# Self-attention softmax: row sums by TensorE over unnormalised exponentials, scaling moved behind the value products

## The reference

```
Q, K, V = x @ w.T + bias, split into heads
S = einsum('hid,hjd->hij', K, Q) * 32 ** -0.5
delta = i - j
S = where(delta < 0, -inf, S) - delta
C = softmax(S, axis=-1)
attn = einsum('hij,hjd->hid', C, V)
out = attn @ o_w.T + o_b
```

## Time and profile before

| | us |
|---|---|
| time, median of 3 runs | 1968.17 (1965.84 to 1968.95) |
| profiled execution, its own time | 1968.37 |
| profiled execution, span | 1966.6 |
| TensorE busy | 1904.0 (97%) |
| VectorE busy | 1099.3 (56%) |
| ScalarE busy | 978.7 (50%) |
| GpSimd busy | 327.6 (17%) |

### The profile page before, as it was taken

One profiled execution on the slowest core, in us unless ns is written; L12 is line 12 of the kernel. 1 busy time (PEld: TensorE's weight loads), 2 busy tenths in 40 slices (PEclk: granted clock), 3 DMA queues, 4 the chain that ended last, 5 costly groups with the idle time before them and its releaser, 6 DMA issues. The chain is left out here.

```text
span 1966.6 us, 32109 instructions
## 1 busy us (share of the span) xinstructions
PE 1904.0 (97%) x10494; PEld 1596.6 (81%) x10494; DVE 1099.3 (56%) x2447; ACT 978.7 (50%) x2079; POOL 327.6 (17%) x238
## 2 busy tenths in 40 slices
PE   9999999999999989999999999999887899999998
PEld 6787888888888878878888888887665688999997
DVE  3567677677677756676776777676645631000003
ACT  3204676676576582055775775775645441122111
POOL 0300211211211213002112111211552300000001
PEclk9999999999999999999999999999999999999999
DMA  7651111111111145501111111111300907577552
GB/s 245 212 193 43 40 50 41 46 37 40 51 32 43 43 150 190 185 25 46 33 45 45 32 49 42 37 38 38 115 15 24 343 6 266 208 265 265 198 188 66
DMA packets 123281, 198.12 MB, mean 101 GB/s; under 512 B 12741, under 2 KB 62021, under 8 KB 119104
## 3 DMA queue, kind: packets, MB, share of 16 engines
q1 hardware_dynamic: 119040, 188.59, 28.8%
q10 hardware_dynamic: 2880, 4.55, 0.7%
q0 software_dynamic: 1280, 3.93, 0.6%
HBM read 151.50 MB, written 45.81 MB: 100 GB/s over the span
## 5 line engine op out<-in xcount | busy, mean ns | idle before, releaser
L861 DVE TENSOR_TENSOR crs_ptl<-crs_tp,crs_pth 128x512 fp32r<-128x512 f32 x512 | 352.7, 689 | 178.9 <-ACT crs_pth L688 178.2
L688 ACT ACTIVATE crs_pth<-crs_tp 128x512 fp32r<-128x512 f32 x504 | 301.6, 599 | 243.7 <-PE crs_tp L1088 240.6
L606 POOL TENSOR_TENSOR crs_vl<-crs_vraw,crs_vh 128x512 fp32r<-128x512 f32 x128 | 164.9, 1288 | 1072.6 <-ACT crs_vh L695 1072.6
L1079 PE MATMUL crs_ring<-crs_kh,crs_ql 128*128 128x512 f32 x512 | 234.0, 457 | 0.3 <-DVE crs_kl L865 0.3
L1098 PE MATMUL crs_ov<-crs_ptl,crs_vh 128*128 128x512 f32 x512 | 209.6, 409 | 9.3 <-DVE crs_ptl L861 7.0
L1079 PE MATMUL crs_ring<-crs_kh,crs_qh 128*128 128x512 f32 x512 | 202.2, 395 | 0.0
L1098 PE MATMUL crs_ov<-crs_pth,crs_vh 128*128 128x512 f32 x512 | 202.2, 395 | 0.0
L1079 PE MATMUL crs_ring<-crs_kl,crs_qh 128*128 128x512 f32 x512 | 201.2, 393 | 0.0
L1098 PE MATMUL crs_ov<-crs_pth,crs_vl 128*128 128x512 f32 x512 | 199.3, 389 | 0.0
L1088 PEld LDWEIGHTS crs_tp<-all_ident,crs_prob 128*128 128x128 f32 x1024 | 143.0, 140 | 68.8 <-ACT crs_more L677 4.2
L1088 PE MATMUL crs_tp<-all_ident,crs_prob 128*128 128x128 f32 x1024 | 195.0, 272 | 3.3 <-ACT crs_more L677 3.3
(11 more groups left out here) (284 smaller groups left out, 3337.1 us busy)
## 6 DMA issues: line engine op xcount, KB each, us to landing
moe_w<-in_L_ffn_w SPq DMA_DIRECT2D x48, 1024.0 KB, 12.8
v_scratch<-crs_more SPq DMA_DIRECT2D x64, 512.0 KB, 2.9
crs_vraw<-v_scratch SPq DMA_DIRECT2D x128, 256.0 KB, 2.8
ex_w<-in_L_ffn_w SPq DMA_DIRECT2D x16, 1024.0 KB, 13.8
crs_prob<-in_ctx SPq DMA_DIRECT2D x16, 512.0 KB, 4.6
crs_wo<-in_L_xattn_Wo SPq DMA_DIRECT2D x16, 512.0 KB, 4.1
moe_w<-in_L_ffn_sw SPq DMA_DIRECT2D x8, 1024.0 KB, 13.4
qry_wq<-in_L_xattn_Wq SPq DMA_DIRECT2D x16, 256.0 KB, 4.1
```

Source lines behind the costliest of these rows:

```text
L606: nc.gpsimd.tensor_tensor(vl[:, n % VR, :, :], vraw[:, :, :], vh[:, n % VR, :, :].bitcast(F32), ALU.subtract).then_inc(s["v_lo"], 1)
L688: act.activation(pth[:, k % PT, :], tp[k % PT][:, :], ACT.Copy).then_inc(s["pt_hi"], 1)
L861: v.tensor_tensor(ptl[:, k % PT, :], tp[k % PT][:, :], pth[:, k % PT, :].bitcast(F32), ALU.subtract).then_inc(s["pt_lo"], 1)
L1079: m = pe.matmul(ring[at % RING][:, :], a[:, t // RT, rows], w[:, n % KR, :], start=i == 0, stop=i == 2)
```

## The change

The exponentials are turned and multiplied with V as they are, without their norm. Their sums are made by TensorE: behind the value products of a half come the same products with a matrix of ones in place of V, in the same column tiles, into the other half of the output's bank (`r_ps`), so that each sum stands in all 32 rows of its head. `inverse`, `normalise` and the accumulator of the exponentials go. VectorE's new `output` takes the reciprocal of `r_ps` (128x256) and multiplies `o_ps` with it into `on`. ScalarE copies `on` to `oh`, and GpSimd makes `ol`. TensorE's transposes wait for the exponentials, and its value products for `output` of the index before.

```diff
+        ones = t.sb("ones", [P, HW])
+        rinv = t.sb("rinv", [P, RT, P])
+        on = [t.sb(f"on{q}", [P, RT, P]) for q in range(2)]
+
+        r_ps = o_bank[:, TQ:2 * TQ].rearrange("p (r n) -> p r n", r=RT)
...
+            nc.gpsimd.memset(ones[:, :], 1.0).then_inc(c, 1)
+            pool.wait_ge(c, 2)
...
-            def normalise(n, it):
-                heads = HC // (it + 1)
-                pool.wait_ge(s["inv_ok"], unit(n, it))
-                w = sc[n % 2][it][:, 0:heads, :]
-                nc.gpsimd.tensor_tensor(w, w, rsum[n % 2][it][:, 0:heads].unsqueeze(2).to_broadcast([P, heads, (it + 1) * P]), ALU.mult).then_inc(s["norm_ok"], 1)
-
             for n in range(N):
-                for it in range(RT):
-                    normalise(n, it)
+                pool.wait_ge(s["o_hi"], n + 1)
+                nc.gpsimd.tensor_tensor(ol[:, place(n), :, :], on[n % 2][:, :, :], oh[:, place(n), :, :].bitcast(F32), ALU.subtract).then_inc(s["o_lo"], 1)
...
-            def inverse(n, it):
-                v.wait_ge(s["exp_ok"], unit(n, it))
-                v.reciprocal(rsum[n % 2][it][:, :], rsum[n % 2][it][:, :]).then_inc(s["inv_ok"], 1)
-                if it == 1:
-                    v.wait_ge(s["inv_ok"], unit(n, it))
-                    w = sc[n % 2][it][:, HC // 2:HC, :]
-                    v.tensor_tensor(w, w, rsum[n % 2][it][:, HC // 2:HC].unsqueeze(2).to_broadcast([P, HC // 2, 2 * P]), ALU.mult).then_inc(s["norm2_ok"], 1)
-
-            def output_low(n):
-                v.wait_ge(s["o_hi"], n + 1)
-                v.tensor_tensor(ol[:, place(n), :, :], o_ps, oh[:, place(n), :, :].bitcast(F32), ALU.subtract).then_inc(s["o_lo"], 1)
+            def output(n):
+                v.wait_ge(s["o_ps"], unit(n, 1) * HC)
+                v.reciprocal(rinv[:, :, :], r_ps).then_inc(s["inv_ok"], 1)
+                v.wait_ge(s["inv_ok"], n + 1)
+                if n >= 2:
+
+                    v.wait_ge(s["o_lo"], n - 1)
+                v.tensor_tensor(on[n % 2][:, :, :], o_ps, rinv[:, :, :], ALU.mult).then_inc(s["norm_ok"], 1)
...
             scores(0, 0)
             scores(0, 1)
-            inverse(0, 0)
             for n in range(N):
                 if n < N - 1:
                     scores(n + 1, 0)
-                inverse(n, 1)
                 if n < N - 1:
                     scores(n + 1, 1)
-                    inverse(n + 1, 0)
                 if n in QUERY_BESIDE:
                     query(QUERY_BESIDE[n])
                 turned(n)
                 if n:
-                    output_low(n - 1)
+                    output(n - 1)
             residual(0)
-            output_low(N - 1)
+            output(N - 1)
             residual(1)
...
-                    m = act.activation(w, w, ACT.Exp, bias=nmax[n % 2][it][:, h:h + 1], accum_out=rsum[n % 2][it][:, h:h + 1])
+                    m = act.activation(w, w, ACT.Exp, bias=nmax[n % 2][it][:, h:h + 1])
...
             def output_high(n):
-                act.wait_ge(s["o_ps"], unit(n, 1) * HC)
-                act.activation(oh[:, place(n), :, :], o_ps, ACT.Copy).then_inc(s["o_hi"], 1)
+                act.wait_ge(s["norm_ok"], n + 1)
+                act.activation(oh[:, place(n), :, :], on[n % 2][:, :, :], ACT.Copy).then_inc(s["o_hi"], 1)
...
             def transposes(n, it):
-                pe.wait_ge(s["norm_ok"], unit(n, it))
-                if it == 1:
-                    pe.wait_ge(s["norm2_ok"], n + 1)
+                pe.wait_ge(s["exp_ok"], unit(n, it))
...
                 elif n:
-                    pe.wait_ge(s["o_lo"], n)
+                    pe.wait_ge(s["norm_ok"], n)
                 for j in range(it + 1):
                     for h in range(HC):
                         rows = slice(h * HW, (h + 1) * HW)
-                        m = pe.matmul(o_ps[rows, it, :], V[:, place(n), j, rows], cT[n % 2][it][:, j, h * P:(h + 1) * P], start=j == 0, stop=j == it)
+                        pe.matmul(o_ps[rows, it, :], V[:, place(n), j, rows], cT[n % 2][it][:, j, h * P:(h + 1) * P], start=j == 0, stop=j == it)
+                for j in range(it + 1):
+                    for h in range(HC):
+                        rows = slice(h * HW, (h + 1) * HW)
+                        m = pe.matmul(r_ps[rows, it, :], ones[:, :], cT[n % 2][it][:, j, h * P:(h + 1) * P], start=j == 0, stop=j == it)
                         if j == it:
                             m.then_inc(s["o_ps"], 1)
```

More of the change, by code:

```diff
@@ L1201, in selfattn @@
         sc = [[t.sb(f"sc{q}{i}", [P, HC, (i + 1) * P]) for i in range(RT)] for q in range(2)]
-        mx, nmax, rsum = ([[t.sb(f"{n}{q}{i}", [P, HC]) for i in range(RT)] for q in range(2)] for n in ("mx", "nmax", "rsum"))
+        mx, nmax = ([[t.sb(f"{n}{q}{i}", [P, HC]) for i in range(RT)] for q in range(2)] for n in ("mx", "nmax"))
         cT = [[t.sb(f"cT{q}{i}", [P, i + 1, HC * P]) for i in range(RT)] for q in range(2)]
@@ L1221, in selfattn @@
         names = ("var_ready", "root_ready", "xn_ready", "chain", "consts", "b_ld", "vo_ld", "wo_ld", "xT_ps", "xT_hi", "xT_lo", "w_hi", "w_lo",
-                 "q_ps", "q_ok", "k_ps", "k_ok", "v_ps", "v_ok", "xb_ok", "s_ps", "s_ok", "max_ok", "exp_ok", "inv_ok", "norm_ok", "norm2_ok",
+                 "q_ps", "q_ok", "k_ps", "k_ok", "v_ps", "v_ok", "xb_ok", "s_ps", "s_ok", "max_ok", "exp_ok", "inv_ok", "norm_ok",
                  "t_ps", "cT_ok", "cT2_ok", "o_ps", "o_hi", "o_lo", "out_ps", "out_ok")
@@ L1251, in _ @@
             nc.gpsimd.iota(decay[:, :, :], pattern=[[-P, RT], [1, TQ]], base=0, channel_multiplier=-1, allow_small_or_imprecise_dtypes=True).then_inc(c, 1)
-            pool.wait_ge(c, 1)
+            nc.gpsimd.memset(ones[:, :], 1.0).then_inc(c, 1)
+            pool.wait_ge(c, 2)
             nc.gpsimd.affine_select(out=decay[:, :, :], in_=decay[:, :, :], compare_op=ALU.is_ge, fill=NEG,
@@ L1311, in _ @@
             query(1)
-            v.wait_ge(s["consts"], 2)
+            v.wait_ge(s["consts"], 3)
             def scores(n, it):
```

## The result

The changed kernel takes 2008.87 us (median of 4 runs, 2007.20 to 2011.87) against 1968.41 us of the kernel before on the same chip: 1.0203 of its time, with a 95% interval of 1.0185 to 1.0220. The profiled execution took 2009.26 us with a span of 2007.5, 40.9 us more than that of the kernel before.

What follows compares the result with a forecast made beforehand. Self-attention was taken as bound by a chain between engines, none full. Loops +17.3, loop 0 -1.6, the end +1.4 and clock restarts +9.0 gave +26.1 on 1968.37 us: 1994.5, forecast 1994, range 1979 to 2001.

Steps and rivals of the forecast that it cites:

- the moved wait: ScalarE's `output_high(n-1)` now waits for VectorE's `output(n-1)`, behind `turned(n)`, with exponentials queued after it; said to decide.
- the ring: Self-attention loops: transposes, VectorE's output, `output_high`, exponentials, next transposes in one cycle; 64.6 us against 47.3, +17.3.
- 1.16 from the eight transposes to VectorE's copy: Time in each loop from TensorE's transposes (n, 1) to VectorE's `turned(n)`, claimed as 1.16 us.
- 0.28 us each: ScalarE's exponentials of 256 columns without the accumulator read: four in 1.12 us in place of 1.99.
- Six restarts: TensorE at its slow clock after idling in each turn from loop 2 on: six times 1.5 = 9.0 us.
- the reciprocal at 1.7 us: R, VectorE's reciprocal of 128x256 in `output`: 1.7 us from 6 ns a column, bounds 0.42 and 2.7 us.
- what stands behind `out(0)`: After `out(0)`: last index's sums 0.6 us and `out(2)` waiting some 0.8 us for the last output, +1.4.
- Rival (a): VectorE's reciprocal streams at 0.42 us and four clock restarts stay: +13.3, 1982 us; chance 0.20.
- Rival (b): VectorE's reciprocal costs 8 to 10 ns a column, 2.3 to 2.7 us: 1999 to 2002 us; chance 0.11.
- Rival (c): TensorE's clock stays at its upper level although it pauses: 1985.5 us; chance 0.10.
- Rival (e): TensorE's sums run one tile at a time, not four: 14.4 us more, 2008 us; chance 0.02.
- Rival (d): `output_high(n-1)` finds `norm_ok` already given, so loops last as long as TensorE's own work: 1965 us; chance 0.04.

Runs made afterwards that it cites:

- the bare wait: Kernel before plus one wait only: ScalarE's `output_high(n-1)` also waits until VectorE's `turned(n)` is done; 1988.44 us, 1.0100 of before.
- the reorderings: Changed kernel with ScalarE's `output_high(n-1)` behind `turned(n, 1)` and `key`: 1981.58 us; or VectorE's `output(n-1)` ahead of `turned(n)`, `query` last: 1982.59 us; or both: 1971.68 us.
- the run with the copy: Changed kernel with the reciprocal of 128x256 replaced by a copy of the same shape, outputs multiplied by the sums; 1998.61 us, 1.0140 of before.
- both reorderings: Changed kernel with VectorE's `output(n-1)` ahead of `turned(n)`, `query` last, and ScalarE's `output_high(n-1)` behind `turned(n, 1)` and `key`; 1971.68 us, 1.0017 of before.

## Why the prediction was wrong

Direction and mechanism were right: the moved wait decides, `output_high` waits for VectorE's output, and the ring is the one written out. The kernel with the bare wait and the reorderings show it from both sides. The size was not: +26.1 forecast, +40.9 in the profiled executions. What failed are terms of the sum. By step the missing 14.8 us are as follows; this is a comparison of the sum with the trace, and the run with `query` moved warns that a term taken away need not come back in the total:

- **VectorE's place in the ring.** The term "1.16 from the eight transposes to VectorE's copy" was taken from loop 4, which has no `query`. In loops 1 and 3 `query` stands ahead of `turned` and waits for the second half projection; 3.35 us in place of 1.16, 4.4 us over the two. The description of VectorE's order ahead of the prediction had `query` there. The run with `query` moved shows the 2.0 us in loop 1's turn, and nothing in the total.
- **Exponentials.** 0.28 us each, the lower bound, was taken; they cost 0.40 (1467.83 to 1469.42 for four). Six turns of 4 x 0.12: 2.8 us. The rows of copies were of another kind of instruction; halfway between the bounds would have been closer. The Trainium skill ("ScalarE: Activation LUTs", "Step-by-step: what each stage is for") gives 0.833 ns an element whatever the function. This trace agrees for the slope: four of 128 columns start 1.19 us ahead of the next instruction (1459.38 to 1460.57), four of 256 1.59, so 0.10 us for 128 columns.
- **The clock.** Six restarts were counted at 1.5 us. The two turns behind a key pay for the scores too (1.59 us at 1482.35 where they take 0.87), so they are nearer 2.2; together 1.5 us more. The seventh restart, at `out(0)`, was put at nothing without a reason: the last loop was summed to `out(0)`, and its pause (4.15 us) not carried into the clock. It cost 2.1 us (5.15 against 3.00).
- **Behind the stage.** The next stage starts 38.6 us later, the whole kernel ends 40.9 us later. 2.3 us are in the experts, whose instructions are the same, and whose slow stretches of the clock fall elsewhere (granted clock of 0.81 in 1676 to 1691 us, 0.89 at the same place before, 1636 to 1651). Why they fall elsewhere stays open. The changed kernel's group of the first expert products:

```profile
L2141 PE MATMUL moe_bank<-moe_bufT,moe_w 128*128 128x160 f32 x1024 | 146.4, 303 | 0.6 <-ACT moe_bufT L1973 0.6
```

The same group of the kernel before:

```profile
L2144 PE MATMUL moe_bank<-moe_bufT,moe_w 128*128 128x160 f32 x1024 | 145.3, 302 | 0.7 <-ACT moe_bufT L1976 0.7
```

- **The rest.** Loop 0 won 1.15 and not 1.6 us. 4.4 + 2.8 + 1.5 + 2.1 + 2.3 + 0.45 = 13.6; the remaining 1.2 us are small differences spread over the turns (the sums 0.66 us for 0.6, `output_high` 0.32 us ahead of the exponentials for 0.28).

Right were: the reciprocal at 1.7 us (1748 ns) from a difference of 12 ns between two tiny rows, which is luck in part, since rows of two columns scatter from 158 to 166 ns; the multiplication (424 ns for 0.41); the sums at full clock (0.66 for 0.6); the subtraction (724 for 742); what stands behind `out(0)` (+1.6 for +1.4); the slow clock in each turn from loop 2 on. The reading of the Trainium skill's repeat count ("VectorE: DVE Perf Modes", "First, the fixed hardware budget") as 2.3 us for the reciprocal is not borne out: 1748 ns. Rival (a), a streaming reciprocal, is the run with the copy, 1999 and not the 1982 of its sum, for the same missing terms. It also took an idle of 1.7 us for one that leaves the clock up, where the earlier trace rows shows that for 1.43 only; a pause of 1.51 us in the kernel with both reorderings was followed by the lower clock. Rival (b) asked for R above 2.3 and has the wrong cause. Rival (c), a clock that stays up, falls with the 0.67 to 0.87 granted. Rival (e), at 2008, has almost the measured time by accident: the sums take 0.66 us beside the value products' 0.79, so they do not run one tile at a time. Rival (d), the open ring at 1965, had its point right: with `norm_ok` given in time the loops cost what they did (47.45 for 47.28 us). It takes two changes of order, a changed end and four matmuls without use to get to 1965.18.

The range failed for the same reason as the sum. Its ends came from the prices (R, the clock), and no term stood for an instruction that is queued ahead in the ring in some loops only.

## What to carry to other kernels

When an instruction gets a later releaser, move it behind everything in its queue that does not need it, before any price is counted: here one copy of 0.42 us, left ahead of the exponentials, cost 27 of 40 us. Write out such a ring once for each kind of loop, with each engine's whole list in it, and not once from the turn that has the fewest instructions. Carry each pause that the ring makes into TensorE's clock, the last included: all seven of the changed kernel (4.15 to 5.52 us) were followed by a restart. And don't add up small savings of TensorE's work inside a stretch that runs at the lower clock.

## What the runs showed of the hardware

- A reciprocal of 128x256 from PSUM costs 1748 ns, a copy of the same shape 416. With 166 ns for 2 columns the reciprocal comes to some 6.2 ns a column.
- A saving of TensorE's work behind a pause may bring nothing: the first four matmuls of the half projection of loop 2 took 1.20 us in one kernel, 2.06 and 2.08 in the two in which it started sooner behind the restart.
- The length of a pause alone does not tell whether the lower clock follows. A pause of 1.51 us, ahead of transposes (7, 0) of the kernel with both reorderings, was followed by it some 0.6 us into the work, while 1.43 us was not:

```profile
1498.34 0.63 PE L1498 MATMUL att_turn<-all_ident,att_sc 128*128 128x128 f32 x4 [1.51 <-ACT att_cT L1397]
1498.89 0.66 PE L1510 MATMUL att_o<-att_cT,att_V 128*32 128x128 f32 x8
```

Eight value products take 0.43 us at the upper level (1458.61 above). In the kernel with VectorE's output moved ahead of turned, a pause of 3.16 us was not followed by it: the value products are at full speed, and the granted clock is 1.00 in 1501.76 to 1505.00.

```profile
1501.76 0.63 PE L1498 MATMUL att_turn<-all_ident,att_sc 128*128 128x128 f32 x4 [3.16 <-ACT att_cT L1397]
1502.32 0.43 PE L1510 MATMUL att_o<-att_cT,att_V 128*32 128x128 f32 x8
```
